# Layer norm of two dense stages by chunk, scaled on ScalarE; keys and values of all blocks ahead of the queries

## The reference, cut to what matters

```python
def _layernorm(x, axis=-1, eps=1e-05):
    m = jnp.mean(x, axis=axis, keepdims=True)
    v = jnp.var(x, axis=axis, keepdims=True)
    return (x - m) / jnp.sqrt(v + eps)
...
h = jnp.maximum(_layernorm(x, axis=-1), 0.0)
x = x + _L0_gnn_ref(h, edge_index, edge_weight, ...)   # two rounds of sums over edges
h = jnp.maximum(_layernorm(x, axis=-1), 0.0)
x = x + _L1_gnn_ref(h, edge_index, edge_attr_64, ...)  # attention, 4 heads: h @ W_node.T, scores, softmax by target
h = jnp.maximum(_layernorm(x, axis=-1), 0.0)
x = x + _L2_gnn_ref(h, ..., src, dst)                  # attention, 8 heads: q, k, v = h @ W.T + b
h = jnp.maximum(_layernorm(x, axis=-1), 0.0)
x = x + _L3_gnn_ref(h, edge_index, ...)                # two rounds of gated sums
```

## Time and profile before

| | us |
|---|---|
| median of 3 runs | 4066.55 (4063.19 to 4077.22) |
| profiled execution, its own time | 4065.1 |
| its span in the profile | 4063.3 |
| POOL busy | 2775.2 (68% of the span) |
| PE, DVE, ACT busy | 1921.5, 1821.7, 1086.3 |
| mean granted TensorE clock | 0.659 of 2.4 GHz |

### The profile page before, as it was taken

The page is one execution under the profiler, slowest core; times in us unless marked ns, Lnnn a source line. Parts: engine busy times, 40 slices in busy tenths (PEclk is TensorE's granted clock), DMA queues, the critical chain, the costliest instruction groups (busy, mean ns, idle before and its releaser), DMA issues. The chain is left out here.

```text
span 4063.3 us, 45249 instructions
## 1 busy us (share of the span) xinstructions
PE 1921.5 (47%) x10431; PEld 1699.2 (42%) x10432; DVE 1821.7 (45%) x4393; ACT 1086.3 (27%) x3123; POOL 2775.2 (68%) x2907
## 2 busy tenths in 40 slices
PE   7630016666543333456676455555633333433332
PEld 7620015555443333356665345555433333333332
DVE  8990047777643221335555757777721110311111
ACT  3110002223300000267777267777400000000000
POOL 5777777777567777277777077777167777477775
PEclk9995556766666655655656677877655655656655
DMA  4100012122222222333333244444221222311223
GB/s 129 50 11 12 3 39 53 53 52 53 38 60 53 52 53 52 48 83 81 80 80 69 39 138 130 132 130 123 24 59 53 52 53 52 48 53 52 53 53 55
DMA packets 147256, 254.57 MB, mean 63 GB/s; under 512 B 58965, under 2 KB 82932, under 8 KB 146857
## 3 DMA queue, kind: packets, MB, share of 16 engines
q0 software_dynamic: 99328, 193.52, 20.7%
q1 hardware_dynamic: 43354, 47.14, 4.0%
q10 hardware_dynamic: 4430, 12.43, 0.9%
HBM read 236.59 MB, written 16.30 MB: 62 GB/s over the span
## 5 line engine op out<-in xcount | busy, mean ns | idle before, releaser
L603 POOL DMA_INDIRECT arena<-tab_dram,tblk x832 | 792.4, 952 | 415.6 <-issue 252.9
L603 POOL DMA_INDIRECT pool<-tab_dram,tblk x816 | 774.5, 949 | 426.3 <-issue 247.7
L1133 PE MATMUL psum<-pool 128*128 128x128 f32 x1344 | 313.1, 427 | 555.5 <-DMA pool<-tab_dram,tblk 550.5
L1133 PEld LDWEIGHTS psum<-pool 128*128 128x128 f32 x1344 | 290.8, 328 | 579.3 <-issue 579.3
L603 POOL DMA_INDIRECT ACC<-tab_dram,tblk x432 | 407.5, 943 | 131.7 <-issue 131.7
L580 POOL DMA_INDIRECT rec_dram<-arena,ACC x400 | 391.0, 977 | 154.0 <-issue 120.7
L603 POOL DMA_INDIRECT pool<-tab_dram,arena x416 | 400.6, 963 | 131.8 <-issue 126.5
L1110 PE MATMUL psum<-pool 128*128 128x128 f32 x832 | 192.9, 426 | 450.4 <-DMA pool<-tab_dram,arena 366.7
L1110 PEld LDWEIGHTS psum<-pool 128*128 128x128 f32 x832 | 180.0, 328 | 454.8 <-issue 276.7
L1188 PE MATMUL psum<-pool 128*128 128x136 f32 (+1 forms) x1664 | 321.5, 366 | 45.8 <-DVE pool L1802 41.3
L1188 PEld LDWEIGHTS psum<-pool 128*128 128x128 f32 x1664 | 298.4, 262 | 57.6 <-issue 30.5
(11 more groups left out here) (303 smaller groups left out, 3952.8 us busy)
## 6 DMA issues: line engine op xcount, KB each, us to landing
pool<-dst_dram SPq DMA_DIRECT2D x104, 256.0 KB, 3.5
arena<-tab_dram,tblk POOLq DMA_INDIRECT x832
pool<-tab_dram,tblk POOLq DMA_INDIRECT x816, 2.5
HN<-in_edge_attr_dram ACTq DMA_DIRECT2D x23, 500.0 KB
ACC<-tab_dram,tblk POOLq DMA_INDIRECT x432, 2.5
pool<-tab_dram,arena POOLq DMA_INDIRECT x416
rec_dram<-arena,ACC POOLq DMA_INDIRECT x400
tab_dram<-arena SPq DMA_DIRECT2D x24, 256.0 KB
```

The costliest lines, as they stand in the source:

```text
L603: nc.gpsimd.indirect_dma_start(to[:, j, :], None, tab_dram[k], bass.IndirectOffsetOnAxis(ap=idx[:, G * g + j:G * g + j + 1], axis=0)).then ...
L1133: last = nc.tensor.matmul(psum[:, bass.ds(vals[j] * P, P)], row if k in FLIPPED else one, one if k in FLIPPED else row, start=False, stop= ...
```

## The change: what it does

In stages 3 and 4 the norm goes chunk by chunk. `spread_of` takes the place of `norm_stats`: `bn_aggr` signals `s_var` for each block, ACT takes the root of four variances with eps as its bias (`rooted`), DVE forms the reciprocal and -mean times the reciprocal of the chunk (`inverse`), one chunk later in its list, and ACT normalises the blocks by scale and shift per row (`scaled`). ACT's flows get two lanes more. In stage 4 `products` multiplies by keys and values only, two blocks to a bank, and DVE takes out two blocks with one instruction; the new `queries` follows when DVE has taken out all of these, four blocks to a bank, and DVE takes four blocks of queries out with one instruction.

```diff
+            def rooted(stage):
+                def work(c, n):
+                    lo, hi = 4 * c, 4 * c + n
+                    act.wait_ge(s_var, NB * (LNS[stage] - 1) + hi)
+                    nc.scalar.activation(stat[:, 3, lo:hi], meanvar[:, lo:hi, 1], ACT.Sqrt, bias=epsilon[:, 0:1]).then_inc(s_root, 1)
...
+            def scaled(stage):
+                def work(c, n):
+                    act.wait_ge(s_shift, CHUNKS * (LNS[stage] - 1) + c + 1)
+                    for b in range(4 * c, 4 * c + n):
+                        nc.scalar.activation(HN[:, b, :], X[:, b, :], ACT.Identity, scale=stat[:, 4, b:b + 1], bias=stat[:, 5, b:b + 1]).then_inc(s_normed, 1)
...
-            root()
-            flow((0, turned(3, ACT.Relu)), (1, only(0, root)), (1, made(3)))
+            flow((0, rooted(3)), (1, scaled(3)), (2, turned(3, ACT.Relu)), (3, made(3)))
             part_pass(2)
             answer(stat[:, 4:8, :].rearrange("p h b -> p b h"), m3[:, :, 0:4], ACT.Exp, scale=-1.0)
-            root()
-            flow((0, turned(4, ACT.Relu)), (1, only(0, root)))
+            flow((0, rooted(4)), (1, scaled(4)), (2, turned(4, ACT.Relu)))
...
                 pe.wait_ge(s_ft, before(4, c, TURNED) + 1)
-                for b in range(4 * c, 4 * c + n):
-                    if b >= 4:
-                        pe.wait_ge(s_q, b - 3)
-                        pe.wait_ge(s_kv, b - 3)
-                    nc.tensor.matmul(bank[4 + b % 4][:, 0:3 * D], FT[:, b * P:(b + 1) * P], wT[:, 1:4, :].rearrange("p a f -> p (a f)"),
+                for h in range(0, n, 2):
+                    r = 2 * c + h // 2
+                    if r >= 4:
+                        pe.wait_ge(s_kv, r - 3)
+                    for q in range(min(2, n - h)):
+                        b = 4 * c + h + q
+                        last = nc.tensor.matmul(bank[4 + r % 4][:, 2 * D * q:2 * D * (q + 1)], FT[:, b * P:(b + 1) * P],
+                                                wT[:, 2:4, :].rearrange("p a f -> p (a f)"), start=True, stop=True)
+                    last.then_inc(s_qkv, 1)
+            def queries():
+                pe.wait_ge(s_kv, 2 * CHUNKS - 1)
+                for c, n in T_CH:
+                    if c >= 4:
+                        pe.wait_ge(s_q, c - 3)
...
+            def inverse(which, c, n):
+                lo, hi = 4 * c, 4 * c + n
+                dve.wait_ge(s_root, CHUNKS * which + c + 1)
+                link(v.reciprocal(stat[:, 4, lo:hi], stat[:, 3, lo:hi]))
+                v.scalar_tensor_tensor(stat[:, 5, lo:hi], meanvar[:, lo:hi, 0], -1.0, stat[:, 4, lo:hi], ALU.mult, ALU.mult).then_inc(s_shift, 1)
+            def spread_of(which, c, n):
+                if c:
+                    inverse(which, c - 1, 4)
+                for b in range(4 * c, 4 * c + n):
+                    queued(v.bn_stats(lnst[:, b, :], X[:, b, :]))
+                dve.wait_ge(s_dve, done[0])
+                for b in range(4 * c, 4 * c + n):
+                    v.bn_aggr(meanvar[:, b, :], lnst[:, b, :]).then_inc(s_var, 1)
+                if c == CHUNKS - 1:
+                    inverse(which, c, n)
...
             flow((0, add_divided))
-            for b in range(NB):
-                dve.wait_ge(s_qkv, b + 1)
-                v.scalar_tensor_tensor(HN[:, b, :], bank[4 + b % 4][:, 0:D], 0.25, bqkv[:, 0, :], ALU.mult, ALU.add).then_inc(s_q, 1)
-                v.tensor_tensor(QKV[:, b, D:3 * D], bank[4 + b % 4][:, D:3 * D], bqkv[:, 1:3, :].rearrange("p a f -> p (a f)"), ALU.add).then_inc(s_kv, 1)
+            for c, n in T_CH:
+                for h in range(0, n, 2):
+                    r, m = 2 * c + h // 2, min(2, n - h)
+                    dve.wait_ge(s_qkv, r + 1)
+                    v.tensor_tensor(QKV[:, 4 * c + h:4 * c + h + m, D:3 * D], bank[4 + r % 4][:, 0:2 * D * m].rearrange("p (b f) -> p b f", b=m),
...
```

More of the change, by code:

```diff
@@ L179, in gnn_kernel @@
         bnv = sb("bnv", [P, 8])
+        epsilon = sb("epsilon", [P, 1])
         hist = sb("hist", [P, 2, NB])
@@ L345, in gnn_kernel @@
         s_normed = sem("s_normed")
+        s_var = sem("s_var")
+        s_root = sem("s_root")
+        s_shift = sem("s_shift")
         s_nodes = sem("s_nodes")
@@ L532, in _ @@
                     if k == 3:
-                        sp.wait_ge(s_kv, 4 * c + n)
+                        sp.wait_ge(s_kv, 2 * c + (n + 1) // 2)
                     else:
@@ L663, in work @@
                                          bias=bgb[:, stage - 6:stage - 5]).then_inc(s_side_read, 1)
+                return work
+            def rooted(stage):
[3 more added lines that the diff above has]
+                    nc.scalar.activation(stat[:, 3, lo:hi], meanvar[:, lo:hi, 1], ACT.Sqrt, bias=epsilon[:, 0:1]).then_inc(s_root, 1)
+                return work
+            def scaled(stage):
[3 more added lines that the diff above has]
+                        nc.scalar.activation(HN[:, b, :], X[:, b, :], ACT.Identity, scale=stat[:, 4, b:b + 1], bias=stat[:, 5, b:b + 1]).then_inc(s_normed, 1)
                 return work
@@ L984, in products @@
                 pe.wait_ge(s_ft, before(4, c, TURNED) + 1)
-                for b in range(4 * c, 4 * c + n):
-                    if b >= 4:
-                        pe.wait_ge(s_q, b - 3)
-                        pe.wait_ge(s_kv, b - 3)
-                    nc.tensor.matmul(bank[4 + b % 4][:, 0:3 * D], FT[:, b * P:(b + 1) * P], wT[:, 1:4, :].rearrange("p a f -> p (a f)"),
-                                     start=True, stop=True).then_inc(s_qkv, 1)
+                for h in range(0, n, 2):
[12 more added lines that the diff above has]
+                        pe.wait_ge(s_q, c - 3)
+                    for q in range(n):
+                        b = 4 * c + q
+                        last = nc.tensor.matmul(bank[4 + c % 4][:, q * D:(q + 1) * D], FT[:, b * P:(b + 1) * P], wT[:, 1, :], start=True, stop=True)
+                    last.then_inc(s_qkv, 1)
             def prefixes():
@@ L1235, in _ @@
             flow((0, turn(4)), (1, products))
-            pe.wait_ge(s_q, NB)
-            pe.wait_ge(s_kv, NB)
+            queries()
+            pe.wait_ge(s_q, CHUNKS)
             part_pass(3)
@@ L1279, in _ @@
             link(v.memset(ue2[:, :], 0.0))
+            link(v.memset(epsilon[:, :], EPS))
             link(v.memset(X[:, NB - 1, :], 0.0))
@@ L1428, in _, with norm_stats @@
             ft3 = FT[:, :].rearrange("p (b f) -> p b f", b=NB)
-            def norm_stats(c, n):
+            def norm_stats(c, n, half=HALF):
                 for b in range(4 * c, 4 * c + n):
@@ L1436, in norm_stats @@
                     queued(v.bn_aggr(meanvar[:, b, :], lnst[:, b, :]))
-                if c + 1 == HALF:
-                    norm_ask(0, 4 * HALF)
+                if c + 1 == half:
+                    norm_ask(0, 4 * half)
                 elif c + 1 == CHUNKS:
-                    norm_ask(4 * HALF, NB)
-                if c == HALF:
-                    norm_answer(0, 4 * HALF)
+                    norm_ask(4 * half, NB)
+                if c == half:
+                    norm_answer(0, 4 * half)
                 elif c + 1 == CHUNKS:
-                    norm_answer(4 * HALF, NB)
+                    norm_answer(4 * half, NB)
             def norm_ask(lo, hi):
@@ L1474, in work @@
                     dve.wait_ge(s_taken, before(stage, c, MADE) + 1)
-                    norm_stats(c, n)
+                    if stage == 2:
+                        spread_of(0, c, n)
+                    else:
+                        norm_stats(c, n)
                 return work
@@ L2005, in add_divided @@
                 link(v.tensor_tensor(chunk_of(X, c, n), chunk_of(X, c, n), chunk_of(HN, c, n), ALU.add))
-                norm_stats(c, n)
+                spread_of(1, c, n)
             flow((0, add_divided))
-            for b in range(NB):
-                dve.wait_ge(s_qkv, b + 1)
-                v.scalar_tensor_tensor(HN[:, b, :], bank[4 + b % 4][:, 0:D], 0.25, bqkv[:, 0, :], ALU.mult, ALU.add).then_inc(s_q, 1)
-                v.tensor_tensor(QKV[:, b, D:3 * D], bank[4 + b % 4][:, D:3 * D], bqkv[:, 1:3, :].rearrange("p a f -> p (a f)"), ALU.add).then_inc(s_kv, 1)
+            for c, n in T_CH:
[3 more added lines that the diff above has]
+                    v.tensor_tensor(QKV[:, 4 * c + h:4 * c + h + m, D:3 * D], bank[4 + r % 4][:, 0:2 * D * m].rearrange("p (b f) -> p b f", b=m),
+                                    bqkv[:, 1:3, :].rearrange("p a f -> p (a f)").unsqueeze(1).to_broadcast([P, m, 2 * D]), ALU.add).then_inc(s_kv, 1)
+            for c, n in T_CH:
+                dve.wait_ge(s_qkv, 2 * CHUNKS - 1 + c + 1)
+                v.scalar_tensor_tensor(chunk_of(HN, c, n), bank[4 + c % 4][:, 0:n * D].rearrange("p (b f) -> p b f", b=n), 0.25,
+                                       bqkv[:, 0, :].unsqueeze(1).to_broadcast([P, n, D]), ALU.mult, ALU.add).then_inc(s_q, 1)
             total = part_pass(3)
```

## The result

| | before | after |
|---|---|---|
| median of 9 runs each | 4066.55 us (4061.99 to 4077.22) | 4056.50 us (4049.34 to 4063.11) |
| profiled execution, own time / span | 4065.1 / 4063.3 | 4057.71 / 4055.9 |
| mean granted TensorE clock | 0.659 | 0.653 |

By the medians it is 10.05 us (0.25%) faster, where 4054.8 us was forecast. The two profiled executions differ by 7.4 us of span.

What follows compares the result with a forecast made beforehand. When POOL may issue its gathers bounds the kernel, so dense stages are paid in full. From the profiled 4065.1 us, +0.8 (stage 3), -11.3 (stage 4) and +0.2 (new constant, rounding) gave 4054.8 us; range 4048 to 4064.

Steps and rivals of the forecast that it cites:

- Stage 4, -11.3 forecast: Stage 4: the last take of keys and values and the store behind it come earlier, 11.3 us off the kernel.
- First take: Stage 4: DVE takes out its first product 20.2 us after the stage's start, against 24.9 before.
- The last take: Stage 4: DVE's last take of keys and values ends at 30.0 us against 41.5, at 2.16 us a chunk.
- rival 2: PE's clock stays low through stage 3 (+12) or falls in stage 4's idle stretch (+8): 4062 to 4067 us; chance 0.11.
- Stores and queries, nothing forecast: End of stage 4: no store queues (bound +1.5 us), and queries hide before DVE's first use of gathered rows.
- Stage 3, +0.8 forecast: Stage 3: ACT's order gives back DVE's gain, -0.2 us, and PE's clock adds 1.0; bounds -1.5 and +12 us.
- the root of chunk 3 is queued behind that take: Stage 3, ACT's queue: that root follows the take of the first turned chunk, so DVE waits some 2.5 us.
- PE's clock ... so I put the rise a little later and add 1 us: Stage 3: earlier but thinner PE work makes the rise to 2.4 GHz a little later, costing 1 us.
- a sign against it (PE at 1.2 GHz from 1698): Stage 3: PE at 1.2 GHz from 1698 on would show the prediction wrong; before, it was at 2.4 GHz from 1698.
- The scaling, 0.30 forecast: ACT's normalising of blocks in stages 3 and 4: 0.30 us a block, 1.2 us a chunk.
- The first (stage 3 gains too): Stage 3 gives 1.5 to 2.5 us, with PE at 2.4 GHz and cheaper scalings: 4051.8 us; chance 0.38.
- The third: ACT reloads its table between root and Identity or ReLU in both stages: 4085 us; chance 0.04, with a low clock.

Runs made afterwards that it cites:

- the split only: The kernel before with stage 4's keys and values of all blocks ahead of the queries, norm left on DVE in both stages; 4060.7 us, ratio 0.9976.

## Why the prediction was right, and where it was off

**Stage 4, -11.3 forecast.** Measured -9.9 in the first profile and -11.4 in the second of the same kernel. First take forecast at 20.2, measured 20.12, with DVE's wait for the last root 1.23 where about 1.0 was forecast; the norm's half was to give 4.7 and gives 4.8; PE's pace of 2.16 us a chunk shows in the products' starts at 2.4 GHz (2320.66 to 2322.83, 2.17). The last take was forecast at 30.0: it is at 30.1 where the clock held and 31.7 where it fell at PE's idle stretch, near the +2 that stood under rival 2. The extra products, which fill that stretch, bring 30.1. The Trainium skill (TensorE: Matmul & The Clock Gate, What's actually happening) says that the same kernel shows different numbers of slow matmuls from run to run; these two profiles agree, with the eight products behind the idle stretch in 3.55 us in the one and 1.97 in the other, and 37.84 and 36.37 us to the gather.

**Stores and queries, nothing forecast.** From the last store to the gather it is 6.0 us (2327.72 to 2333.73), 6.2 before, so no stores queue. DVE has its sums cleared at 2337.77 and gets its first gathered rows at 2345.69, so 7.9 us are left, 9 forecast, and the queries cost nothing.

**Stage 3, +0.8 forecast, +4.2 measured.** The step "the root of chunk 3 is queued behind that take" was right, with 2.37 us for "some 2.5", and the kernel with later takes shows it by taking it away. The term that was mis-sized is "PE's clock ... so I put the rise a little later and add 1 us". The rise that lasted came not a little later but 15 us (1712.5, before 1697.9), with a short one at 1705.7. Its price shows in two places. Extra products that brought the rise forward took 3.5 us off DVE's waits at chunks 5 and 6, and the copy then came at +21.8, where the prediction had 22.0 without its clock term. And from the first copy to the gather it is 19.6 us after and 18.6 before: the five profiles in which the clock was down once more behind the copy have 19.6 to 20.0, the eight others 18.2 to 18.6. Together that is some 4.5 us for the term that was put at 1. The reason given, that PE's work would be thinner, is not in the rows either: in 1694 to 1698 PE was busy 4.00 us at 1.2 GHz, and before it was busy 3.38 us and the clock rose behind it. This is also what the prediction named as a sign against it (PE at 1.2 GHz from 1698). The scaling, 0.30 forecast by a biased square of the earlier trace rows, is 0.41 a block, which makes ACT's slot 0.4 us longer; with a constant scale the copy is still at +25.6, so at this clock this term shows no effect on the end.

**The rivals.** The first (stage 3 gains too) did not come. The kernel with later takes shows that 1.2 us were there, but by another order, not by a cheaper scaling. The second, the low clock, came in part: some 4.5 us in stage 3 and 1.5 in one profile of stage 4, 6 us where the rival needed 7 to 12. What the prediction held against it, that both stages had 2.4 GHz for most of their length, misreads the trace of before: it was 17 of stage 3's 41 us (1697.9 to 1714.9) and 24 of stage 4's 48. The third is out: the one load in the timeline is at 2294.18, behind the Exp and ahead of stage 4, as before; the Trainium skill (ScalarE: Activation LUTs, Table sets: the hidden batching unit) has the cheap functions in every set, and the trace agrees, with no load in either stage.

**The total** is nearer than its terms, and that is luck. Stage 3 was 3.4 us worse and stage 4 0.0 to 1.4, and the median is 1.7 us above the forecast. The sum started at the profiled execution, so it forecast 10.3 us off that one, and 7.4 came; the median of before lies 1.45 us higher. What made up the rest lies in code that the change leaves alone. The first gather of pass 5 follows a dense stage in which POOL waits 39.16 us before, 37.45 after, 35.09 with stage 4 changed only, 45.35 with stage 3 changed only, and 45.08 with the split only. The windows over the middle of that stage, of the kernel with stage 4 changed only, then with stage 3 changed only, show the clock:

```profile
3477.00:3489.00 12.00, 9.83 (x53) 6.23 (x53) 10.02 (x17) 6.01 (x12) 0.00 (x0) 0.85 0.07 22
```

```profile
3503.00:3515.00 12.00, 12.00 (x43) 9.35 (x42) 5.84 (x14) 3.57 (x8) 0.00 (x0) 0.50 0.22 66
```

That is 10 us between kernels whose code there is the same, as much as the change is worth. Whether the change moves it, or each execution falls one way or the other, was not tried. The changed kernel's two profiles have 37.45 and 37.58, which speaks for the kernel. For the execution speaks that the twelve runs of the kernel with stage 3 changed only lie in two groups of six, 4062.9 to 4068.9 us and 4075.7 to 4080.6, with the profiled one, which has the 45.35 us, in the upper. It stays open, and single profiles of these kernels should not be compared by their whole time.

## What to carry to other kernels

When statistics are sent from one engine to another and back per chunk, write down the receiving engine's queue: a root behind a take that waits for a third engine held DVE at each of the last four chunks of stage 3, 9.3 us together, and one lane more between root and take brought the first copy forward by 4.1 us. In stage 4, where ACT has no second take in its slot, the same order cost one wait of 1.23 us at the end. Output that the next phase needs first (keys and values) can go ahead of the rest whenever the rest fits in the time until its first use; that half was worth 6.6 us with as many columns of product as before. Short stages of matmuls between long phases are to be costed at both of TensorE's clock levels: the low one was worth some 4.5 us in stage 3, 1.5 in stage 4 and about 10 in a stage whose code was the same.

## What was not expected of the hardware

- A scale per row makes ACT's 128x128 Identity 479 ns, beside 388 with a constant scale and the same bias per row.
- PE idled 3.76 us in stage 4 before and the clock held. Of the seven profiles of the changed stage 4 without extra products there, the clock fell in the four in which it had risen by +14.9 and PE idled 3.4 to 3.8 us, and held in the three in which it rose at +15.7 or later and PE idled 2.6 to 2.8 us. With before beside them, the length of the idle stretch does not decide it by itself; what does stays open.
- Extra products ahead of stage 3 had the clock at 2.4 GHz for the stage's turns in one kernel; in the other, with ACT's takes a lane later, it was down again at 2076.6, before DVE had its root of chunk 4.
- By the profile's account PE can be busy all the time and stay at 1.2 GHz: 4.00 of 4.00 us in stage 3 after, 12.00 of 12.00 us ahead of pass 5 with stage 3 changed only. The busy time of such a row does not tell its clock.
- One chip ran the kernel before in 5049.6 us instead of some 4066. The added time lay in the passes, none in the dense stages; its cause was not looked for.
